# Where batch 1's h is split, how unit 0 is transposed and when the residual is added in a two-layer cross-attention kernel

## The reference

```python
h = layer_norm(x, scale, offset)
q = h @ wq + bq;  k = ctx @ wk + bk;  v = ctx @ wv + bv      # + one learned key and value
ctx_out = softmax(q @ k.T / sqrt(128)) @ v
x = x + ctx_out @ wo + bo                                    # twice, with weights of its own
h = layer_norm(x, scale, offset)
out = x + gelu(h @ w_fc1 + b_fc1) @ w_fc2 + b_fc2            # 256 -> 1024 -> 256
```

## Time and profile before

| | us |
|---|---|
| median of 3 runs | 513.48 (513.2 to 514.86) |
| the profiled execution | 513.09 |
| its span, first to last instruction | 511.3 |
| PE busy | 492.6 (96%) |
| DVE busy | 400.5 (78%) |
| POOL busy | 409.6 (80%) |
| ACT busy | 331.9 (65%) |

### The profile page before, as it was taken

The page is one execution under the profiler, slowest core; times in us unless marked ns, Lnnn a source line. Parts: engine busy times, 40 slices in busy tenths (PEclk is TensorE's granted clock), DMA queues, the critical chain, the costliest instruction groups (busy, mean ns, idle before and its releaser), DMA issues.

```text
span 511.3 us, 10944 instructions
## 1 busy us (share of the span) xinstructions
PE 492.6 (96%) x3219; PEld 446.3 (87%) x3219; DVE 400.5 (78%) x918; ACT 331.9 (65%) x723; POOL 409.6 (80%) x374
## 2 busy tenths in 40 slices
PE   8798999999999999999978999999999999999887
PEld 6687899999989998999967899998999899999877
DVE  4989788887887888856798878788788788866783
ACT  3567767776775767675366867667676666677231
POOL 5747998989898998985596998989989898987630
PEclk9989999999999999999999999999999999999989
DMA  8418866656667576602118866676757665610101
GB/s 279 128 62 257 268 200 195 196 180 208 182 205 226 169 238 186 200 30 63 62 49 274 255 200 185 201 196 205 214 175 228 191 195 196 194 43 2 42 1 42
DMA packets 54181, 84.66 MB, mean 166 GB/s; under 512 B 6010, under 2 KB 34830, under 8 KB 54158
## 3 DMA queue, kind: packets, MB, share of 16 engines
q1 hardware_dynamic: 54158, 84.38, 54.0%
HBM read 54.47 MB, written 29.88 MB: 165 GB/s over the span
## 4 chain that ended last, share of the span: by engine, by line
PE 86%; DVE 7%; POOL 3%; issue 1%; DMA 1%; ACT 1%; SPq 0%; DVEq 0%; POOLq 0%
PE ring L1118 64%; PE ps_ctx L1118 10%; PE acc L1118 10%; DVE k_lo L780 1%; DVE h_lo L905 1%; DMA x_sb<-x_in 1%; PE ring L1158 1%; DVE blocks L819 1%; DVE z_sb L885 1%; POOL v_lo L387 1%; POOL wf_lo L334 1%; DVE k_lo L1106 0%; DVE pT_lo L832 0%; DVE bn L874 0%; DVE h_full L896 0%
## 5 line engine op out<-in xcount | busy, mean ns | idle before, releaser
L847 DVE TENSOR_REDUCE row_max<-ring 128x1 f32<-128x512 f32 x112 | 76.6, 689 | 30.8 <-PE ring L1118 30.7
L592 ACT ACTIVATE probs<-ring,shift 128x512 f32<-128x512 f32 x112 | 76.4, 682 | 18.5 <-DVE shift L852 18.4
L387 POOL TENSOR_TENSOR v_lo<-v_sum,v_hi 128x512 fp32r<-128x512 f32 x64 | 83.1, 1301 | 2.6 <-ACT v_hi L550 2.5
L394 POOL TENSOR_SCALAR probs<-probs,inv 128x512 f32<-128x512 f32 x80 | 55.3, 696 | 32.9 <-DVE inv L860 32.8
L819 DVE STREAM_TRANSPOSE blocks<-probs 128x512 f32<-128x512 f32 x112 | 72.6, 687 | 0.8 <-POOL probs L394 0.4
L399 POOL TENSOR_TENSOR pT_lo<-wf_lo,pT_hi 128x1024 fp32r<-128x1024 f32 x28 | 66.9, 2409 | 0.0
L1118 PE MATMUL ring<-pT_lo,v_hi 128*128 128x256 f32 x208 | 58.6, 282 | 4.0 <-DVE k_lo L780 3.2
L532 ACT ACTIVATE k_hi<-ring,cols 128x512 fp32r<-128x512 f32 x57 | 37.7, 689 | 34.8 <-PE ring L1118 34.7
L1118 PE MATMUL ring<-pT_hi,v_lo 128*128 128x256 f32 x208 | 58.0, 279 | 0.0
L1118 PE MATMUL ring<-pT_hi,v_hi 128*128 128x256 f32 x208 | 58.0, 279 | 0.0
L1118 PE MATMUL ring<-wv_lo,cT_hi 128*128 128x256 f32 x196 | 54.9, 280 | 0.0
(11 more groups left out here) (179 smaller groups left out, 1639.2 us busy)
## 6 DMA issues: line engine op xcount, KB each, us to landing
spill<-blocks SPq DMA_DIRECT2D x56, 512.0 KB, 2.9
wf_hi<-spill SPq DMA_DIRECT2D x112, 128.0 KB, 3.2
wf_lo<-spill SPq DMA_DIRECT2D x112, 128.0 KB, 3.3
wk_raw<-wk_in SPq DMA_DIRECT2D x17, 256.0 KB, 2.8
wq_raw<-wq_in SPq DMA_DIRECT2D x17, 256.0 KB, 3.7
wv_raw<-wv_in SPq DMA_DIRECT2D x16, 256.0 KB, 3.8
vrows<-vrows_in SPq DMA_DIRECT2D x16, 256.0 KB, 4.1
wo_raw<-wo_in SPq DMA_DIRECT2D x16, 256.0 KB, 2.7
```

The lines of the kernel that those rows point to most:

```text
L387: pool.tensor_tensor(v_lo[:, 2 * m:2 * m + 2, :], v_sum[:, m % 2, :].rearrange("p (t c) -> p t c", c=PW), v_hi[:, 2 * m:2 * m + 2, :].bitc ...
L394: pool.tensor_scalar(probs[:, u, q, :], probs[:, u, q, :], inv[:, u, q:q + 1], 0.0, ALU.mult, ALU.add).then_inc(p_ready_pool, 1)
L592: act.activation(probs[:, u, q, :], ring[S_BANKS[where][QTB * u + q]][:], ACT.Exp, bias=shift[:, u, q:q + 1], scale=SCALE, accum_out=row_s ...
L847: dve.reduce_max(row_max[:, u, q:q + 1], ring[S_BANKS[where][QTB * u + q]][:], AX_X).then_inc(max_done, 1)
```

## The change

- Batch 1's h of both layers: ACT scales it out of PSUM (`drain_h`, now for layer 1 too), POOL takes h_lo (`split_late_h`, in the prologue) under a semaphore of its own; DVE's `split_h(layer, 1)` and `scale_h(layer, 1)` are gone.
- `residual` is four instructions of 128x256. It moves from the first step to the last step of the same layer, in front of POOL's wait for `outputs_done`. For the MLP it moves behind a wait for the rest of hidden tile 11.
- Unit 0 of a first step is transposed by PE (`transpose_first`), rounded by ACT straight from PSUM (`round_first`) and its rest taken by DVE (`split_first`); its block transpose, its write, its read, `round_moved` and `moved_rest` are gone. The banks of the first step are dealt anew. Unit 3's block transpose on DVE moves behind the four `split_k`.
- The prologue: POOL waits until z is done before it splits wk; in layer 1 `inverse_deviation` stands before the split of MLP part 0, and MLP part 1 is split inside the first step. `clear_acc` of layer 0 moves to the warm-up, in place of two of its six matmuls. PE's wait for z is by tile.
- The MLP: the first two hidden tiles take the products with h_hi first (`hidden_first`); the transposes of batch 1's z move one tile forward; POOL splits parts 4 and 5 after batch 1's h_lo instead of after z.

```diff
-V_BANKS = {"first": [None, None, 3, 2], ...
-K_BANKS = {"first": [5, 2, 3, 4], ...
+V_BANKS = {"first": [None, None, 3, 0], ...
+K_BANKS = {"first": [4, 1, 5, 3], ...
-Q_BANKS = {"first": [1, 0], "step": [3, 4]}
+Q_BANKS = {"first": [2, 3], "step": [3, 4]}
+FIRST_PT_BANKS = [1, 5]
...
 SP:
                 for half in range(2):
-                    for u in (2 * half, 2 * half + 1):
+                    units = [u for u in (2 * half, 2 * half + 1) if u > 0 or not first]
+                    for u in units:
                         write_blocks(pair, layer, u, first)
-                    for u in (2 * half, 2 * half + 1):
+                    for u in units:
                         read_blocks(pair, layer, u, first)
...
 POOL:
-                rows = out_rows[:, norm:norm + 1, :].to_broadcast([P, QT, D])
-                pool.tensor_tensor(x_res[:], x_sb[:], rows, ALU.add).then_inc(res_ready, 1)
+                for t in range(QT):
+                    added = pool.tensor_tensor(x_res[:, t, :], x_sb[:, t, :], out_rows[:, norm, :], ALU.add)
+                added.then_inc(res_ready, 1)
+            def split_late_h(layer):
+                for c in range(DC):
+                    pool.wait_ge(h_rounded, DC * (BATCH * layer + 1) + c + 1)
+                    last = pool.tensor_tensor(h_lo[:, c, QLEN:], h_full[:, c, QLEN:], h_hi[:, c, QLEN:].bitcast(F32), ALU.subtract)
+                last.then_inc(h_split_late, 1)
...
                     inverse_deviation(0, 1)
+                    pool.wait_ge(z_ready, QT)
                     pool.wait_ge(k_filled, NK)
                     split_wk(1)
+                    split_late_h(0)
+                    value_rest(0, 0)
                 else:
-                    pool.wait_ge(h_split, BATCH * layer + 1)
-                    split_mlp(0)
                     inverse_deviation(layer, 1)
                     pool.wait_ge(z_ready, QT * layer + QT)
-                    split_mlp(1)
+                    split_mlp(0)
+                    value_rest(first, 0)
+                    split_late_h(layer)
                     pool.wait_ge(k_filled, NK * (first + 1))
                     split_wk(first + 1)
-                value_rest(first, 0)
                 value_rest(first, 1)
...
             def first_step(pair, layer):
-                residual(layer)
                 normalise(pair, 0, [0, 1])
                 next_wq(pair - 1, layer)
                 value_rest(pair, 2)
                 normalise(pair, 1, [1])
+                if layer > 0:
+                    split_mlp(1)
                 normalise(pair, 2, [0, 1])
...
 (last_step)
                 normalise(pair, 2, [0])
+                residual(layer)
                 pool.wait_ge(outputs_done, layer + 1)
                 split_wo(pair)
                 normalise(pair, 2, [1])
...
 (MLP)
-            pool.wait_ge(z_ready, QT * NORMS)
+            pool.wait_ge(h_split, LAYERS + 2)
             split_mlp(4)
             split_mlp(5)
+            pool.wait_ge(g_split, NG - 4)
             residual(LAYERS)
...
 ACT, first_step:
                 exponential(pair, 3, 1, "first", layer, first=True)
+                round_first(pair, layer, 0)
+                round_first(pair, layer, 1)
                 round_q(pair + 1, 1, "first", layer)
...
-                round_moved(pair, layer, 0, first=True)
...
 DVE, first_step:
                 shifts(pair, 0, 0)
-                split_h(layer, 1)
                 maximum(pair, 0, 1, "first")
...
-                transpose_blocks(pair, layer, 0, first=True)
                 shifts(pair, 2, 1)
...
+                split_q(pair + 1, 0, "first", layer)
                 sum_v(pair, 3, "first")
-                split_q(pair + 1, 0, "first", layer)
+                split_first(pair, layer, 0)
                 inverse_sums(pair, 3)
+                split_first(pair, layer, 1)
                 split_q(pair + 1, 1, "first", layer)
                 transpose_blocks(pair, layer, 2, first=True)
                 split_k(pair + 1, 0, "first")
-                transpose_blocks(pair, layer, 3, first=True)
                 split_k(pair + 1, 1, "first")
-                moved_rest(pair, layer, 0)
                 split_k(pair + 1, 2, "first")
                 split_k(pair + 1, 3, "first")
+                transpose_blocks(pair, layer, 3, first=True)
...
 PE, first_step:
-                pe.wait_ge(h_split, BATCH * layer + 2)
+                pe.wait_ge(h_split_late, layer + 1)
                 project_first_q(0, 1, layer)
...
                 scores(3, 1, "first")
+                pe.wait_ge(p_ready_pool, NORMS_POOL * pair + 1)
+                transpose_first(0, layer)
+                pe.wait_ge(p_ready_pool, NORMS_POOL * pair + 2)
+                pe.wait_ge(exp_done, NS * pair + 4)
+                transpose_first(1, layer)
                 pe.wait_ge(wq_split, pair + 2)
+                pe.wait_ge(exp_done, NS * pair + 5)
                 project_q(0, "first")
...
 PE, step:
-                pe.wait_ge(q_split, NQ * (pair + layer + 2))
-                pe.wait_ge(v_summed, NV * (pair - 1) + 3)
+                pe.wait_ge(q_split, NQ * (pair + layer + 1) + 1)
+                pe.wait_ge(v_summed, NV * pair)
                 scores(0, 0, "step")
-                pe.wait_ge(v_summed, NV * pair)
+                pe.wait_ge(k_split, NK * pair + 2)
                 scores(0, 1, "step")
...
 PE, MLP:
+            def hidden_first():
+                ...
+                for c in range(DC):
+                    pe.wait_ge(h_rounded, DC * BATCH * LAYERS + c + 1)
+                    (w_hi h_hi and w_lo h_hi of both tiles)
+                pe.wait_ge(h_split, LAYERS + 1)
+                (w_hi h_lo of both tiles)
...
             keep_warm(KEEP_WARM)
-            pe.wait_ge(h_split, BATCH * LAYERS + 1)
-            for n in range(NG + G_LAG):
-                if n == 6:
+            hidden_first()
+            for n in range(2, NG + G_LAG):
+                if n == 5:
                     transpose_z(LAYERS, 1, "mlp")
                     clear_acc(LAYERS, 1)
```

More of the change, by code:

```diff
@@ L50 @@
 C_BANKS = {"step": [2, 0, 2, 5], "last": [2, 1, 0, 2], "own": [4, 1, 3, 4]}
[L51 to L52 removed]
+V_BANKS = {"first": [None, None, 3, 0], "step": [5, 4, 0, 1], "last": [5, 0, 1, 3], "prologue": [3, 5], "between": [3, 0]}
+K_BANKS = {"first": [4, 1, 5, 3], "step": [1, 3, 2, 3], "last": [2, 2, 1, 5], "prologue": [5, 4, 0, 1]}
 FIRST_Q_BANKS = [2, 4]
[L54 removed]
+Q_BANKS = {"first": [2, 3], "step": [3, 4]}
+FIRST_PT_BANKS = [1, 5]
 PT_BANKS = [3, 1, 4, 0, 3, 0, 5, 0]
@@ L266, in step @@
             def step(pair, layer, first=False, wq=True, wv=True):
+                if first:
+                    if layer > 0:
+                        sp.wait_ge(blocks_ready, NU * (pair - layer))
+                        sp.wait_ge(landed[0], QB * LOAD * (pair - layer))
+                    sp.sem_inc(blocks_ready, 1)
+                    sp.sem_inc(landed[0], QB * LOAD)
+                    sp.sem_inc(spilled[0], LOAD)
                 sp.wait_ge(wk_split, pair + 2)
@@ L811, in transpose_blocks @@
                         dve.wait_ge(spilled[u + 2], LOAD * done)
-                else:
+                elif not first or u == 3:
                     dve.wait_ge(spilled[u - 2], LOAD * (done + 1))
+                elif layer > 0:
+                    dve.wait_ge(spilled[u], LOAD * done)
+                if first and u == 1:
+                    dve.wait_ge(spilled[0], LOAD * (done + 1))
                 if ACT_TILES[u]:
@@ L932, in prologue @@
                     split_k(first, 3, "last")
-                    scale_h(layer, 1, where)
             def first_step(pair, layer):
@@ L1152, in scores, with transpose_first @@
                 product(ring[S_BANKS[where][QTB * u + q]][:], [(*tile, k_hi[:, h, part], k_lo[:, h, part])]).then_inc(s_filled, 1)
+            def transpose_first(q, layer):
+                for t in range(CTB):
+                    last = pe.transpose(ring[FIRST_PT_BANKS[q]][:, t * P:(t + 1) * P], probs[:, 0, q, t * P:(t + 1) * P], ident[:])
+                last.then_inc(first_filled, 1)
             def transpose_own(j):
@@ L1224, in prologue @@
                     project_v(0, where)
-                for b in range(BATCH):
+                for b in range(BATCH if layer > 0 else 0):
                     clear_acc(layer, b)
                 pe.wait_ge(wq_split, first + 1)
-                pe.wait_ge(h_split, BATCH * layer + 1)
+                pe.wait_ge(h_split, layer + 1)
                 for h in range(2):
@@ L1432, in _ @@
             pe.wait_ge(zeros_ready, 1)
-            keep_warm(WARM_UP)
+            keep_warm(WARM_UP - BATCH)
+            for b in range(BATCH):
+                clear_acc(0, b)
             pe.wait_ge(ident_ready, 2)
@@ L1476, in hidden_layer @@
                                                       for c in range(DC)]).then_inc(g_filled, 1)
+            def hidden_first():
+                pe.wait_ge(wk_split, ALL_PAIRS + 1)
```

(11 more changed lines are left out.)

58 lines of the change are left out of this document (37 added, 21 removed).

## The result

The changed kernel takes 507.03 us (median of 4, 505.21 to 508.8) beside 513.34 for the kernel before, run alongside (median of 4, 512.93 to 514.86): a ratio of 0.9871 with a 95% interval of 0.9831 to 0.9912, 6.3 us less. Forecast were 504.3 us in a range of 501.0 to 508.6: faster, as said, by a third less than said. The profiled execution took 505.21 us around a span of 503.4; against that of before, 513.09 and 511.3, it is 7.9 shorter.

A forecast was written before the change was run, and what follows sets the result against it. TensorE, busy 96% of the span, was taken as the bound. Terms: layer 0 -4.65 and 0, layer 1 -1.65 and +1.0, MLP -3.9, sum -9.2; from the median of 513.48 to 504.3 us, range 501.0 to 508.6.

The forecast's parts named there:

- the wait of 1 to 2 us: Before the second step's queries: TensorE would wait 1 to 2 us, with ACT idle on wf_lo's DMA.
- Layer 0: Prologue and first step: waits for z, h_lo and k_lo and the slow clock go, transposes added; gain 4.65 us.
- Layer 1's round trip: Unit 2 through DRAM after the first step: 4.9 us from reads to rounding, bounds 3.9 and 6.9, TensorE waiting 1.45.
- Rival A: Both first steps: the round trip costs less and they keep the 1.78 us; -12.1, 501.4 us; chance 0.13.
- Rival B: Round trip 2 us more, or layer 1's DVE late: +2 in each layer, -5.2, 508.3 us; chance 0.15.
- The clock: Behind the h_lo waits in layer 0 and the MLP: the lower clock's cost, 1.3 us each, goes.
- The last step of layer 1: Residual of 2.7 us in POOL's idle time of 1.66 delays TensorE's own transposes: +1.0 us, bounds 0.7 and 1.3.
- The MLP: Before tile 8: the 2.5 us gap for batch 1's h_lo and 1.3 of clock go; -3.9 us, bounds -2.5 and -4.3.
- Rival C: MLP: casts of tiles 3 and 4, delayed by parts 4 and 5, stop `mlp_output`; -5.3, 508.2 us; chance 0.12.
- Rival E: First steps: the change does nothing because another engine holds the same place; -2.9, 510.6 us; chance 0.04.
- rival D: Loop: a wait for all four v sums recurs 12 times; at 0.9 a pass +1.6, 515.1 us; chance 0.04.

The follow-up runs named there:

- unit0_blocks: Changed kernel with unit 0 of a first step again transposed by blocks and through DRAM, as before the change: 503.09 us, ratio 0.9811.
- ef_mlp_old: exp_first with the whole MLP of the kernel before, residual as one instruction: 505.14 us, ratio 0.9837.
- ef_mlp_res_old: exp_first with the MLP's residual, still four instructions, right behind GpSimd's part 5 instead of at the end: 501.33 us, ratio 0.9788.
- ef_parts_z: exp_first with GpSimd's parts 4 and 5 starting behind z again, residual still behind hidden tile 11: 502.09 us, ratio 0.9795.
- ef_h_on_dve: exp_first with VectorE instead of GpSimd splitting batch 1's h, after its first shifts: 502.09 us, ratio 0.9797.
- exp_first: Changed kernel with ScalarE, in the loop passes, doing unit 1's exponentials before rounding the moved unit 2: 502.16 us, ratio 0.979.
- after_again: The changed kernel run once more with no edit: 507.76 us, ratio 0.9891 to the kernel before.

## Why the prediction was right, and where it was off

**Right in sign, range and mechanism.** The time fell into the range, and most of the marks it named are in the trace: h_lo waits of at most 1.0 us, h_lo on GpSimd at 0.72 each (1.45 for two), k_lo's 1.62 us gone and turned into a wait before the second step's queries with ScalarE idle on wf_lo, a wait of 0.78 at the own transposes of layer 1, k_lo at 0.42. Two marks failed: of the wait of 1 to 2 us one was 2.70, and the granted clock stayed up throughout in 2 of 10 executions of the changed kernel at most, going by their mean clock. Of the 2.7 us by which the median lies above the forecast, 1.3 are terms of the sum, and 1.4 come in because the profile lies 1.8 under the median and not 0.4 as before.

**Layer 0** was forecast at 4.65 and came to 4.61. The pieces: the scores of unit 2 at 25.30 instead of near 25.6; the transposes 0.92 instead of 0.95; the end of the keys at 38.66, where 39.05 was forecast. The reads began at 42.09, 3.43 us behind it, where 3.3 was forecast.

**Layer 1's round trip is the mis-sized term of the profile.** Up to the end of the keys the gain was 1.36 against 1.35. Behind it the sum took 4.9 us for the round trip, from layer 0 alone, and it took 5.91 (it was 279.88 - 273.97). That is 1.0 of the 1.3 us by which the profiled gain fell short. The prediction's bound of 6.9 held it. Rival A, a cheaper trip for less traffic, falls: no trip of the changed kernel was under 5.12. Rival B named what the traces point to, that the reads share the queues with write 3, at more than the price: +2 in each layer, where the profile shows 1.7 in both together; nothing there was late on VectorE. The 28 trips of all profiles divide by it. In the four whose reads began 2.0 to 2.6 us behind unit 3's write (both layers of before and of unit0_blocks) the trip took 4.90, 4.72, 5.04 and at most 4.30 us; in the other 24, with reads 0.5 us behind it, 5.10 to 6.24. The same four are the ones in which unit 0 goes through DRAM too, and no edit kept the write away from the reads and changed nothing else, so this is likely and not shown. Why layer 1's trips (5.53 to 6.24) are longer than layer 0's (5.10 to 5.62) stays open.

**The clock is the missing term of the median.** The sum let the clock stay at its upper level behind a wait of 1.45 us. Behind waits of 1.8 to 3.0 us (those of the two profiles) it falls in most executions, going by their mean clock, at 1.4 to 1.5 us each. The prediction had the rows for this in hand, a fall behind 2.84 and 2.38 us and none behind 2.29, and used them only for what goes; a wait that it had forecast with bounds of up to 3.4 us should have had the fall within its bounds.

**The last step of layer 1** cost 1.01 for a forecast of 1.0, by the count of 2.7 in an idle time of 1.66.

**The MLP** gained 4.13 for 3.9: 2.54 from the start of the MLP to tile 8 and 1.6 behind it, the clock. ef_mlp_old brings the wait back as 2.37 us, so the term is real; its clock part comes in some executions and not in others, and where it doesn't the 3.9 is 2.4. Rival C falls: the casts of the next tiles did take up to 1.38 us instead of 0.28 (after, 484.14) and nobody waited for them. The prediction put the credit too simply, that moving x_res alone buys the time. Either edit of GpSimd's list nearly suffices: with the parts behind h_lo the residual may stand right behind them (ef_mlp_res_old, no wait), with the residual late the parts may start behind z (ef_parts_z, 0.24 us), and with both undone, in four pieces, 0.77 us come back.

On this bears the Trainium skill, "SBUF — State Buffer", section "Who interferes with whom": besides operations with two SBUF operands, a `cast` can go into a mode in which it needs the port pair that it shares with GpSimd. The trace agrees: casts of 128x256 take 0.28 us alone, 1.38 beside GpSimd's splits (after, 484.14) and 0.83 beside its additions (ef_mlp_res_old).

**Credit by part.** The prediction tied the first steps' h_lo to GpSimd doing it at 0.7. ef_h_on_dve shows that VectorE would have done almost as well, with the residual away in layer 0 and an earlier start in layer 1. Rival E, no gain in the first steps, falls with the 4.61 and 1.36 us there. The four-sum wait in the loop, rival D, never showed: no entry of the wait list has more than two places.

## What to carry to other kernels

When a stall is removed from an engine, follow the chain that runs beside it to the next point where both meet, here a DRAM round trip, and look at what stands behind the waiting instruction in its queue: it may need nothing of that, and here two lines exchanged (exp_first) were worth more than the part that laid the chain bare. Give a round trip through DRAM the spread of several, not the one value at hand, and look at what is written just ahead of the reads. And where a forecast wait of TensorE can come near the waits that a fall has followed (2.20 us was the shortest here), put a possible clock fall behind it into the range.

## What was not expected of the hardware

- The granted clock fell to the 1.2 GHz level behind waits of 2.20, 2.38, 2.84 and 3.03 us, and stayed at the 2.4 GHz level behind waits of 1.83, 2.29, 2.37 and 2.70. The wait at one place of one kernel goes either way from one execution to the next (1.83 and 2.20, 2.70 and 3.03), and a longer wait is no sure sign: 2.70 without a fall, 2.20 with one. A fall cost 1.3 to 1.6 us. In after_again each step of 0.003 in the mean clock is about 1.8 us of time, of it 0.3 a longer wait.
- A pair of VectorE subtractions of two 128x256 SBUF operands, 0.75 us alone, took 1.42, 1.86, 2.38 and 4.00 us beside GpSimd. Beside a long instruction it is not a share of a rate but a wait for its end: k_lo, 0.43 alone, took 2.47 beside an addition of 2.42 and ended 0.29 us behind it, and the pair of 4.00 ended 0.29 us behind the residual.
- One wide GpSimd addition took 2.40 to 2.52 us; the same in four pieces took 2.82 beside VectorE instructions with one operand in PSUM (after, 460.32) and up to 3.40 beside its casts and subtractions from SBUF. Pieces let VectorE in between: the pair that shared the stretch with them took 2.38 and not 4.00.
